# Pair attention of a vision tower: output projection, and in the first one queries and keys, as three fp32r products of high and low parts instead of fp32

## The reference

```python
qkv = x @ w_attn + b_attn                       # [32, 37, 256] @ [256, 768]
q, k, v = split(qkv, 3)                         # 16 heads of 16 features each
att = einsum('bhqd,bhkd->bhqk', q, k) * 0.25    # causal mask, softmax over the keys
y = einsum('bhqk,bhkd->bhqd', softmax(att), v)  # back to [32, 37, 256]
h = layernorm(x + (y @ w_proj + b_proj))
```

## Time and profile before

| | us |
|---|---|
| Median of 3 runs | 1152.99 |
| Fastest and slowest of them | 1147.05, 1163.36 |
| The profiled execution | 1149.84 |
| Its span, first to last instruction | 1148.0 |
| PE busy, share of the span | 932.5 (81%) |
| DVE busy | 587.7 (51%) |
| ACT busy | 488.4 (43%) |
| Mean granted TensorE clock | 0.874 of 2.4 GHz |

### The profile page before, as it was taken

The page is one execution under the profiler, slowest core; times in us unless marked ns, Lnnn a source line. Parts: engine busy times, 40 slices in busy tenths (PEclk is TensorE's granted clock), DMA queues, the critical chain, the costliest instruction groups (busy, mean ns, idle before and its releaser), DMA issues. The chain is left out here.

```text
span 1148.0 us, 25356 instructions
## 1 busy us (share of the span) xinstructions
PE 932.5 (81%) x10044; PEld 709.3 (62%) x10044; DVE 587.7 (51%) x1275; ACT 488.4 (43%) x908; POOL 328.0 (29%) x428
## 2 busy tenths in 40 slices
PE   4889857499999799869994599999179999989564
PEld 4878625377777557558873366666067777777332
DVE  3575666456666279744564322122354456432575
ACT  3345557455555289625540122222123334432454
POOL 0211311543442000020231244443345454531101
PEclk9999878698999789889995699999687999986775
DMA  6200030200000100000005952232220000000001
GB/s 188 103 3 2 3 115 1 78 1 2 0 0 1 43 1 1 0 6 2 3 3 205 350 148 47 46 46 29 53 82 3 2 2 3 3 2 2 1 1 43
DMA packets 22842, 46.54 MB, mean 41 GB/s; under 512 B 4575, under 2 KB 14591, under 8 KB 22094
## 3 DMA queue, kind: packets, MB, share of 16 engines
q1 hardware_dynamic: 17550, 37.93, 9.4%
q0 software_dynamic: 5184, 7.08, 3.8%
HBM read 37.75 MB, written 7.25 MB: 39 GB/s over the span
## 5 line engine op out<-in xcount | busy, mean ns | idle before, releaser
L2594 PE MATMUL psum<-L2f_EW,weights_even 128*128 x216 | 102.9, 600 | 0.4 <-ACT weights_even L2365 0.4
L2526 DVE TENSOR_TENSOR weights_even<-psum,weights_even 128x512 f32<-128x512 f32 x27 | 18.7, 691 | 105.7 <-PE psum L2594 105.7
L2332 POOL DMA_INDIRECT expert_sums<-weights_even,L2f_target x27 | 42.8, 1584 | 94.0 <-DVE weights_even L2519 83.7
L1026 PE MATMUL psum<-L_cT,weights_odd 128*128 128x222 f32 (+1 forms) x192 | 48.6, 386 | 9.2 <-DVE L_by_sin L915 8.0
L2594 PEld LDWEIGHTS psum<-L2f_EW,weights_even 128*128 128x128 f32 x216 | 37.5, 193 | 28.0 <-issue 27.9
L2211 PE MATMUL psum<-weights_even,L1f_H 128*111 128x256 f32 x176 | 46.7, 421 | 8.5 <-DVE L1f_H L2142 8.4
L2365 ACT ACTIVATE weights_even<-psum 128x256 f32<-128x256 f32 x27 | 10.4, 384 | 98.0 <-PE psum L2589 98.0
L2627 PEld LDWEIGHTS psum<-L2f_EW,weights_even 128*128 128x128 f32 x216 | 41.0, 190 | 17.6 <-issue 13.4
L2627 PE MATMUL psum<-L2f_EW,weights_even 128*128 x216 | 51.1, 379 | 0.8 <-ACT weights_even L2370 0.8
L915 DVE TENSOR_TENSOR L_by_cos<-psum,vectors_odd 128x444 f32<-128x444 f32 (+1 forms) x48 | 26.5, 552 | 47.9 <-PE psum L1026 47.5
L854 ACT ACTIVATE L_PT<-psum 101x296 f32<-101x296 f32 x32 | 13.3, 417 | 81.5 <-PE psum L1067 80.9
(11 more groups left out here) (429 smaller groups left out, 2512.2 us busy)
## 6 DMA issues: line engine op xcount, KB each, us to landing
L2f_EW<-experts SPq DMA_DIRECT2D x24, 512.0 KB, 13.1
weights_even<-L_w SPq DMA_DIRECT2D x4, 1024.0 KB
patch_ring<-patches SPq DMA_DIRECT2D x11, 333.0 KB, 3.4
weights_odd<-L_wqkv SPq DMA_DIRECT2D x2, 768.0 KB
out<-X SPq DMA_DIRECT2D x10, 111.0 KB
expert_rows<-X SPq DMA_DIRECT2D x1, 1056.0 KB, 5.3
expert_sums<-X SPq DMA_DIRECT2D x1, 1056.0 KB, 17.1
weights_odd<-L_wo SPq DMA_DIRECT2D x1, 1024.0 KB, 8.4
```

The lines of the kernel that those rows point to most:

```text
L1026: mm = nc.tensor.matmul(bank[:, h * NC2:h * NC2 + width(u)], wu[:, (2 * g + h) * 128:(2 * g + h + 1) * 128], cT[:, u % 2, n // 4, 0:width( ...
L2332: nc.gpsimd.indirect_dma_start(sums[:, :], bass.IndirectOffsetOnAxis(ap=target[:, j:j + 1], axis=0), Y[:, j % 2, :], None, compute_op=ALU. ...
L2594: mm = nc.tensor.matmul(core.bank(bank), xsT[:, j % 2, c, :], EW[:, expert[j], first + c * NF:first + (c + 1) * NF], start=c == 0, stop=c ...
```

## The change

The output projection of both attentions is computed by `split_matmul`. ACT's two copies in `o_T` now write a high part `OT_high` (fp32r), and a new DVE function `o_low` reads the same PSUM columns again and writes the difference `OT_low`; `oT_done` is now raised by DVE, behind it. The weights `wo` are split once per stage, high on ACT (L422 in the changed file), low on DVE.

With `parts_of_qk=True`, which only the first attention is given, queries and keys are made the same way: ACT splits the weights first thing in the stage (two copies, L420), and for each unit copies `xT` once more as `x_high` (L380) behind the copy that it already made; DVE makes `x_low` (`x_parts`, L459). `q_project` and `k_project` wait for it. Values are still computed in fp32 from `xT`.

```diff
@@ -254,7 +254,7 @@
     return 8 * (cq % 2) + 2 * (cq // 2) + e
 
 
-def pair_attention(core, name, w, mine, next_loads, next_sem, scale, prep=None, route=None):
+def pair_attention(core, name, w, mine, next_loads, next_sem, scale, prep=None, route=None, parts_of_qk=False):
 
 
 
@@ -284,22 +284,28 @@
         mx = sb("mx", [128, 2, 16])
         rd = sb("rd", [128, 2, 16])
         O = sb("O", [128, 2, 8, 32])
-        OT = sb("OT", [128, 2, B * T])
+        OT = [sb("OT_high", [128, 2, B * T], F32R), sb("OT_low", [128, 2, B * T], F32R)]
+        wo = [sb("wo_high", [128, KD, D], F32R), sb("wo_low", [128, KD, D], F32R)]
+        if parts_of_qk:
+            x2 = [sb("x_high", [128, 2, KD, NC2], F32R), sb("x_low", [128, 2, KD, NC2], F32R)]
+            wqk = [sb("wqk_high", [128, KD, 2 * D], F32R), sb("wqk_low", [128, KD, 2 * D], F32R)]
...
+            x_high, x_low, qk_high, qk_low = st.sems("x_high x_low qk_high qk_low")
...
-        wo = cols(w[f"{name}_wo"], KD, D)
+        whole_o = cols(w[f"{name}_wo"], KD, D)
...
@@ -367,6 +373,11 @@
                                              core.bank(M1)[:, 0:4 * R].rearrange("p (t c r) -> p c t r", t=2, c=KD), ACT.Copy).then_inc(xT_done, 1)
                     else:
...
+                    if parts_of_qk:
+                        act.wait_ge(xT_done, u + 1)
+                        after(act, k_ps, u - 1)
+                        n = width(u)
+                        nc.scalar.activation(x2[0][:, u % 2, :, 0:n], xT[:, u % 2, :, 0:n], ACT.Copy).then_inc(x_high, 1)
 
                 def q_out(u):
                     act.wait_ge(q_ps, u + 1)
@@ -400,11 +411,15 @@
                 def o_T(s):
                     act.wait_ge(oT_ps, s + 1)
                     for b in range(2):
-                        last = nc.scalar.activation(OT[:, :, (2 * s + b) * T:(2 * s + b + 1) * T],
+                        last = nc.scalar.activation(OT[0][:, :, (2 * s + b) * T:(2 * s + b + 1) * T],
                                                     cols(core.bank(OB)[:, 272:480], 2, 104)[:, :, 64 * b:64 * b + T], ACT.Copy)
-                    last.then_inc(oT_done, 1)
-
+                    last.then_inc(oT_high, 1)
+
+                if parts_of_qk:
+                    for n in range(2):
+                        nc.scalar.activation(wqk[0][:, :, n * D:(n + 1) * D], wqkv[:, :, n * D:(n + 1) * D], ACT.Copy).then_inc(qk_high, 1)
                 x_T(0)
+                nc.scalar.activation(wo[0][:], whole_o, ACT.Copy).then_inc(wo_high, 1)
                 q_out(0)
                 k_out(0)
                 for s in range(STEPS):
@@ -437,6 +452,26 @@
...
+                def x_parts(u):
+                    dve.wait_ge(x_high, u + 1)
+                    n = width(u)
+                    nc.vector.tensor_tensor(x2[1][:, u % 2, :, 0:n], xT[:, u % 2, :, 0:n], x2[0][:, u % 2, :, 0:n], ALU.subtract).then_inc(x_low, 1)
+
+                def o_low(s):
+                    dve.wait_ge(oT_high, s + 1)
+                    for b in range(2):
+                        at_ = slice((2 * s + b) * T, (2 * s + b + 1) * T)
+                        last = nc.vector.tensor_tensor(OT[1][:, :, at_], cols(core.bank(OB)[:, 272:480], 2, 104)[:, :, 64 * b:64 * b + T],
+                                                       OT[0][:, :, at_], ALU.subtract)
+                    last.then_inc(oT_done, 1)
+
+                if parts_of_qk:
+                    for n in range(2):
+                        dve.wait_ge(qk_high, n + 1)
+                        part = (slice(None), slice(None), slice(n * D, (n + 1) * D))
+                        nc.vector.tensor_tensor(wqk[1][part], wqkv[part], wqk[0][part], ALU.subtract).then_inc(qk_low, 1)
+                    x_parts(0)
                 for e in range(2):
                     last = nc.vector.tensor_tensor(bkm[:, e], bqk[:, 2:4], parity[:, e:e + 1].broadcast_to([128, 2]), ALU.mult)
                 last.then_inc(set_up, 1)
@@ -492,12 +527,18 @@
 
                 dve.wait_ge(zeroed, 2)
                 v_out(0, 0)
+                dve.wait_ge(wo_high, 1)
+                nc.vector.tensor_tensor(wo[1][:], whole_o, wo[0][:], ALU.subtract).then_inc(wo_low, 1)
                 for s in range(STEPS):
                     u = s // 3
                     if s >= 2:
                         normalise(s - 2)
                     if s < NP:
                         shift(s)
+                    if parts_of_qk and s % 3 == 0 and u + 1 < NU:
+                        x_parts(u + 1)
+                    if s >= 2:
+                        o_low(s - 2)
                     if s == 0:
                         v_out(0, 1)
                     if s % 3 == 1 and u >= 1:
@@ -538,6 +579,16 @@
 
                 def project(u, bank, first, sem):
                     n = width(u)
+                    if parts_of_qk:
+                        pe.wait_ge(qk_low, first // D + 1)
+                        pe.wait_ge(x_low, u + 1)
+                        for c in range(2):
+                            for kd in range(KD):
+                                mm = split_matmul(core, bank[:, c * NC2:c * NC2 + n],
+                                                  [part[:, kd, first + 128 * c:first + 128 * (c + 1)] for part in wqk],
+                                                  [part[:, u % 2, kd, 0:n] for part in x2], kd == 0, kd == KD - 1)
+                        mm.then_inc(sem, 1)
+                        return
                     for c in range(2):
                         for kd in range(KD):
                             mm = nc.tensor.matmul(bank[:, c * NC2:c * NC2 + n], wqkv[:, kd, first + 128 * c:first + 128 * (c + 1)],
@@ -618,13 +669,14 @@
 
                 def o_project(u):
                     pe.wait_ge(oT_done, pairs_of(u + 1))
+                    pe.wait_ge(wo_low, 1)
                     pe.wait_ge(q_done, min(u + 3, NU))
                     after(pe, z_done, u)
                     for m, t in enumerate(UNITS[u][1]):
                         first = min(PER * t, B - PER) * T
                         for c in range(2):
-                            mm = nc.tensor.matmul(core.bank(M2)[:R, m * D:(m + 1) * D], OT[:, c, first:first + R], wo[:, c, :],
-                                                  start=c == 0, stop=c == 1)
+                            mm = split_matmul(core, core.bank(M2)[:R, m * D:(m + 1) * D], [part[:, c, first:first + R] for part in OT],
+                                              [part[:, c, :] for part in wo], c == 0, c == 1)
                     mm.then_inc(y_ps, 1)
 
...
...
-        lambda n: pair_attention(core, "L0", w[n], mine[n], *nxt(n), scale=0.25, prep=prepared["int8"]),
+        lambda n: pair_attention(core, "L0", w[n], mine[n], *nxt(n), scale=0.25, prep=prepared["int8"], parts_of_qk=True),
```

More of the change, by code:

```diff
@@ L293, in pair_attention @@
         (xT_ps, xT_done, q_ps, q_done, k_ps, k_done, v_ps, v_done, s_ps, shifted, exp_done, pt_ps, pt_done, o_ps, o_done,
-         oT_ps, oT_done, y_ps, z_done, var_ready, norm_done, xb_done, zeroed, set_up) = st.sems(
+         oT_ps, oT_done, y_ps, z_done, var_ready, norm_done, xb_done, zeroed, set_up, oT_high, wo_high, wo_low) = st.sems(
             "xT_ps xT_done q_ps q_done k_ps k_done v_ps v_done s_ps shifted exp_done pt_ps pt_done o_ps o_done "
-            "oT_ps oT_done y_ps z_done var_ready norm_done xb_done zeroed set_up")
+            "oT_ps oT_done y_ps z_done var_ready norm_done xb_done zeroed set_up oT_high wo_high wo_low")
+        if parts_of_qk:
+            x_high, x_low, qk_high, qk_low = st.sems("x_high x_low qk_high qk_low")
         if prep:
```

## The result

| us | before | changed |
|---|---|---|
| Median of 4 runs each, taken side by side | 1152.14 | 1177.35 |
| Fastest and slowest | 1147.05, 1163.36 | 1173.16, 1187.76 |
| The profiled execution, its span | 1149.84, 1148.0 | 1177.73, 1175.5 |
| First attention, length | 107.7 | 127.5 |
| Second attention | 110.5 | 112.1 |

The ratio is 1.022, with an interval of 1.012 to 1.032: the change makes the kernel slower, by about 25 us. Forecast were 1168, a range of 1154 to 1184, and "within 2%" as the likeliest class. The time lies in the range, 9 us above the forecast.

What follows compares the result with a forecast made beforehand. PE was taken to bound the first attention, with DVE and ACT forming the chain it waits for. Waits of 19.7 less 4.6 saved on PE, plus 3.0 of clock, made 18.1 on 1149.84: 1168 us, range 1154 to 1184.

Steps and rivals of the forecast that it cites:

- Prices: Both attentions: 0.12 us a record, 0.36 per split product at 222 and 74 columns; 0.62 for a 444-element low part.
- Start +1.9: Start of the first attention: PE's first product at about 46.2 instead of 44.27, behind new copies and low part; +1.9 us.
- step 0 +2.1: First attention, step 0: queries of unit 1 wait for the low part and then the values on DVE; +2.1 us.
- Queries of units 2 to 5, +6.2: First attention, steps 3, 6, 9, 12: queries wait for `x_low`, made behind `shift`; 1.4 each, 2.0 in step 6.
- Output projections +6.0: Both attentions: `o_low` stands between ACT's copies and the projection; 0.5 us in six units, twice.
- late steps +2.7: From step 14 on, values wait for `o_low`; 1.5 us in the first attention, 1.2 in the second.
- rest +0.8: Second attention: `wo_low` moves `shift(0)` by 0.4 us, and `o_low` moves `normalise` by 0.1 in four steps.
- Clock +3.0: TensorE's clock: two more half-clock stretches at 1.5 us each, after the new waits; +3.0 us.
- The waits are covered: Rival: low parts are ready before PE asks, so only PE's -4.6 remains; 1145, up to 1150 us; chance 0.10.
- half of them come back: Rival: ACT and DVE run ahead during waits, leaving 10 us of waits less 4.6; about 1156 us; chance 0.13.
- Four passes to three everywhere: Rival: PE streams a quarter less, 9.6 us saved, with every wait covered; 1140 us; chance 0.02.
- The clock falls for long: Rival: some eight waits each bring half clock and one stretch runs on, adding 12 to 18; 1177 to 1183; chance 0.20.

Runs made afterwards that it cites:

- the kernel with useless products: The changed kernel plus ten fp32 products of 512 columns, results unread, before the waiting queries of the first attention; 1166.49 us, ratio 1.016 to before.
- the repetition: The changed kernel run once more with no edit; 1179.68 us, ratio 1.026 to the kernel before.

## Why the prediction was near, and where it failed

**Bound and chain: right.** That DVE and ACT, busy for little more than half, form the chain that PE's products wait for is what the runs without low parts (1.4 above the line) and with the waits but fp32 products (10.5) show.

**Prices: right.** Two sizes of the parts, 222 and 74 columns, cost 0.11 a record (0.12 forecast), `x_low` 0.62 (0.62), `x_high` 0.57 (0.56); the two records of `OT_low` take 0.37 (0.47). The bound from the 74-column row held. What the products save has to be read from the first of a group to what follows it, on both sides. Four products of the queries took 1.70 before, from 86.16 in the earlier trace rows to

```profile
87.86 0.77 PE L606 MATMUL psum<-L_V,L_PT 101*37 101x34 f32 x32
```

and now take 1.50, from 77.20 to 78.70; those of the keys 1.53 and 1.42. That is 0.04 saved in each product, as forecast. A projection took 1.91 and takes 1.61 (83.19 to 84.80): 0.30 saved, forecast was 0.36.

**Start +1.9, step 0 +2.1: right**, at 1.7 and 2.0 to the start of the queries. **Queries of units 2 to 5, +6.2:** the right waits, slightly oversized. PE waited 1.20 where I had 1.4, and the steps cost 1.15, 1.6 and 1.15 with the saving of the products inside. Start, step 0 and queries less PE's share came to +9.6 in the forecast, and queries and keys alone measured 10.7 +- 0.9. Up to step 12 the scores are 11.2 late: 0.3 is the later start of the stage, about 3.5 the half clock behind the start and step 0, and the other 7.4 stand against 7.6 from the terms of the forecast for these steps.

**Output projections +6.0, late steps +2.7, rest +0.8: near, by the steps.** The 0.50 of wait is there. A step with a projection loses 0.11 or 0.12 in the kernel with the output alone in parts, where 0.5 less 0.36 was forecast. From step 12 to the start of step 15 that kernel loses 2.2 in the first attention (1.5 forecast) and 0.9 in the second (1.2), and `wo_low` costs the second 0.47 (0.4). The second attention is only 1.6 longer all the same, because the half clock of the earlier trace rows at 524.5 is absent in all kernels whose output is in parts, which gives 1.5 back. The changed kernel holds 2.4 GHz from the first products there to the start of step 15:

```profile
525.20:610.30 85.10, 78.47 (x1573) 68.17 (x1571) 55.47 (x128) 42.11 (x110) 18.34 (x24) 1.00 0.01 3
```

By the line the output costs 1.6 +- 0.7 instead of 5.5, and the whole change 10.7 instead of the 15.1 "of waits less saving". The steps do not show where these 4 us are; whether they are in the line or in the forecast stays open.

**Clock +3.0: the term that failed.** Measured is about 17 over the whole kernel by the runs, and the profiles show some 27 us more at half clock within the first attention alone (34.8 and 46.6 against 12.0 and 15.3). The step was "I take two more of them", stretches worth 1.5 each. Two more did come, behind the start and behind step 0, and a third of 3.4 us late in the stage. It missed that the stretch that the earlier trace rows show behind 132 to 135 could become twice as long. I priced waits one by one; but in step 12 several things came together: 0.87 for `L_O` (0.35 before, not in the forecast), 1.09 for `x_low`, and the narrow products, with PE busy for only 2.54 of 4.50. Then the half clock lasted 13.5 us, of which PE's work left no gap, so that every microsecond of it cost half a one, and the narrow products in parts 0.64 each. The two steps took 8.2 longer, where 2.5 was forecast for them without the clock; in the kernel with useless products, which has the same copies and narrow products but no fall there, they took 2.8 longer, 0.86 of it the useless product.

**The number.** 1168 is 9 too low: the clock was 14 larger than its term, and by the line the other terms were 4 smaller. That 1168 came no further off is in part luck, since the two errors point opposite ways, and the time lies in the range because that took in most of the clock's rival. The forecast proper, 1160 to 1175 at 0.55, did not come, and "within 2%" at 0.78 did not hold in the repetition (1.026, 1.021 to 1.031).

**The rivals.** *The waits are covered* and *half of them come back* are out by the 10.7. *Four passes to three everywhere* is out at 74 columns; the products of 222 columns did get cheaper, 0.365 instead of 0.404 each over queries and keys. The Trainium skill ("FP8 and Floating Point Precision", TensorE Precision Notes) counts four passes for true fp32, which makes 0.30 by an estimate of three quarters; the trace does not agree, and stands at the 0.36 of the forecast. *The clock falls for long* (0.20, 1177 to 1183) gave the time that came. Half clock that runs on is what the useless products undid: with them the stage held 2.4 GHz through the same steps. But it did not come at each of eight waits, and the fewer streamed columns that it named aren't needed for it, as the run with fp32 products shows; idle time of PE isn't all of it either, as the run without low parts shows. The row that I set against it, 50 to 60 with 2.4 us idle and no fall, speaks of one stretch, and I let it stand for all.

**What stays open.** Some 19 of the 46 us more at half clock are not in the first attention, and nearly all of them lie in stages whose code is the same. Every variant has more of it (medians of 297 to 329 us) than before has (283), but single profiles of one kernel differ as much: the decay attention took 186.7 and 206.6 in two profiles of the changed kernel. Whether a shifted start of the later stages brings this or chance does, no run here settles. Nor is it settled what of the change brings the half clock in the first attention: taking out either the low parts or the split products of queries and keys leaves 30 or 31 us of it. Not tried were low parts made on POOL, and weight parts prepared in the embedding stage, which would take two copies from the start.

## What to carry to other kernels

Before splitting an fp32 product into cheaper ones, take the price per record at the width at hand: at 222 columns the parts saved a tenth (0.365 against 0.404), at 74 they cost half as much again (0.35 against 0.23), and each operand needs a copy on ACT and a difference on DVE that stand in the chain in front of PE. Price a new wait on a busy TensorE twice, once as idle time and once as half clock behind it, and look at the places where several small waits and narrow products meet: here the longest half clock came behind such a place. And compare variants over many runs with the granted clock of each beside its time: the same kernel ran from 1144 to 1179 us, and its clock explained that with a scatter of 1.3 us.

## What the hardware showed that was not expected

- At 1.2 GHz records of 74, 222 and 256 columns all stand 0.21 apart; at 2.4 GHz they stand 0.11, 0.11 and 0.117 apart. The Trainium skill, "TensorE: Matmul & The Clock Gate", LDWEIGHTS, gives the load of 128 columns of weights as 128 over 1.2 GHz, 0.107; the trace agrees at full clock for 74 and 222 columns, whose records load 128. At half clock the measured 0.21 is twice that: if the load sets the distance, it doubles with the clock; that it does is argued and not shown. A product in three parts costs 0.64 there at all three widths.
- Half clock followed stretches in which PE was busy for 2.54 of 4.50, for 2.72 of 3.80, and, with twelve records of 74 columns at its end, for 3.04 of 3.50.
- Work that nobody reads can shorten a stage: with ten useless products, 8.6 us of PE time, it was 7 to 9 us shorter, and the clock stayed at 2.4 GHz for 82 us on end.
